# The inputs of the point network loaded in four parts behind the batch loop, with the first part's first pass placed among the last batch's gather matmuls

## What is computed

```
idx   = top_k(2 p.p - |p|^2 - |q|^2, 30)          # 30 nearest neighbours of every point
rel   = pts[idx] - pts                            # 3 coordinates, to spherical (rho, theta, phi)
feat  = [sph, sph - mean(sph)]
h     = lrelu(bn(feat @ W1.T)); h = lrelu(bn(h @ W2.T)); h = lrelu(bn(h @ W3.T))
att   = softmax(h[..., 0]);  out = x + sum_k x[idx] * att
```

## Time and profile before

| | |
|---|---|
| median of 3 runs | 7017.76 us (6999.0 to 7027.35) |
| the profiled execution | 6984.93 us, its span 6983.1 us |
| loop ends, last transposes | about 5316 to 5326 us |
| last batch's 12 groups | about 5326 to 5412 us |
| first pass, parts 0 to 2, then part 3 | 5416 to 5484 us, 5513 to 5539 us |
| rest of the network and aggregation | 5539 us to the end |
| PE, DVE busy | 6195.4 us (89%), 6047.0 us (87%) |
| mean granted clock of TensorE | 0.95 |

### The profile page before, as it was taken

One profiled execution on the slowest core, in us unless ns is written; L12 is line 12 of the kernel. 1 busy time (PEld: TensorE's weight loads), 2 busy tenths in 40 slices (PEclk: granted clock), 3 DMA queues, 4 the chain that ended last, 5 costly groups with the idle time before them and its releaser, 6 DMA issues.

```text
span 6983.1 us, 208271 instructions
## 1 busy us (share of the span) xinstructions
PE 6195.4 (89%) x79430; PEld 4459.4 (64%) x79430; DVE 6047.0 (87%) x8509; ACT 4321.9 (62%) x10325; POOL 2693.2 (39%) x3399
## 2 busy tenths in 40 slices
PE   8999999999999999999999999999995795888888
PEld 4666666666666666666666666666664234888878
DVE  6999999989999999999999999999996578777776
ACT  4666666666666666666666666666662156666666
POOL 2444444454444444444444454444443101111110
PEclk9999999999999999999999999999997898999999
DMA  3222222222222222222222222222224003222222
GB/s 118 76 75 72 71 71 68 69 75 80 76 72 78 72 68 68 72 75 76 71 72 68 69 72 83 72 75 75 75 70 133 21 16 76 63 64 62 64 66 59
DMA packets 301388, 499.32 MB, mean 72 GB/s; under 512 B 103859, under 2 KB 217699, under 8 KB 299683
## 3 DMA queue, kind: packets, MB, share of 16 engines
q1 hardware_dynamic: 246733, 389.60, 18.3%
q10 hardware_dynamic: 53589, 95.21, 4.3%
HBM read 410.45 MB, written 74.30 MB: 69 GB/s over the span
## 4 chain that ended last, share of the span: by engine, by line
DVE 41%; PE 29%; issue 21%; DMA 5%; ACT 2%; DVEq 1%; SPq 0%; POOL 0%; ACTq 0%; POOLq 0%
DVE pd L1680 10%; DVE m L1670 9%; DVE idx L1676 8%; PE SCA L901 7%; PE PD L1137 6%; DVE mx L1692 4%; PE SCA L1124 3%; DMA gat<-low_scratch 3%; DVE gat L1624 3%; PE SCB L1124 3%; DVE gat L1994 2%; PE SCB L733 2%; PE SCA L1042 1%; PE SCB L1042 1%; PE TP L1050 1%
## 5 line engine op out<-in xcount | busy, mean ns | idle before, releaser
L1670 DVE MAX8 m<-pd 128x8 f32<-128x1024 f32 x1024 | 1244.3, 1220 | 154.5 <-issue 72.1
L1676 DVE FIND_INDEX8 idx<-m,pd 128x8 uint32<-128x1024 f32 x1024 | 1245.2, 1218 | 0.0
L529 POOL TENSOR_TENSOR prod<-prod,hm 128x480 f32<-128x480 f32 x384 | 396.2, 1032 | 1934.8 <-ACT prod L1310 1923.9
L1680 DVE MATCH_REPLACE8 pd<-m,pd 128x1024 f32<-128x1024 f32 x768 | 928.2, 1209 | 0.4
L1192 ACT ACTIVATE pd<-PD,xxcol 128x512 f32<-128x512 f32 x514 | 368.7, 717 | 722.3 <-PE PD L684 692.3
L708 PEld LDWEIGHTS MISC<-ptab,gat 128*128 128x128 bf16 x23400 | 642.3, 96 | 177.7 <-DVE gat L1624 87.7
L1994 DVE TENSOR_TENSOR gat<-maskT,con 120x2048 f32<-120x2048 f32 x256 | 584.0, 2322 | 166.8 <-PE SCA L1124 164.9
L708 PE MATMUL MISC<-ptab,gat 128*128 128x24 bf16 x23400 | 653.2, 174 | 80.8 <-DVE gat L1624 78.3
L1290 ACT ACTIVATE S<-SCA,mx 128x64 f32<-128x64 f32 (+1 forms) x2560 | 590.1, 406 | 118.7 <-DVE mx L1692 118.3
L1290 ACT ACTIVATE S<-SCB,mx 128x64 f32<-128x64 f32 (+1 forms) x2560 | 580.4, 387 | 19.9 <-DVE mx L1692 19.9
L683 PE MATMUL PD<-arena 128*128 128x512 f32 x1028 | 552.6, 619 | 33.0 <-ACT pd L1192 28.3
(11 more groups left out here) (272 smaller groups left out, 14188.3 us busy)
## 6 DMA issues: line engine op xcount, KB each, us to landing
gat<-low_scratch SPq DMA_DIRECT2D x396, 640.0 KB, 3.9
arena<-in_ctx ACTq DMA_DIRECT2D x33, 512.0 KB, 4.2
x_scratch<-arena ACTq DMA_DIRECT2D x33, 512.0 KB, 3.2
x3T_scratch<-reg ACTq DMA_DIRECT2D x33, 512.0 KB, 3.4
maskT<-in_mask SPq DMA_DIRECT2D x32, 512.0 KB
arena<-in_x ACTq DMA_DIRECT2D x32, 512.0 KB, 4.4
reg<-in_ctx ACTq DMA_DIRECT2D x32, 512.0 KB, 3.5
arena<-x3T_scratch SPq DMA_DIRECT2D x32, 512.0 KB, 6.0
```

Source lines behind the costliest of these rows:

```text
L1670: V.max(m, buf[:, :]).then_inc(found, 1)
L1676: last = V.max_index(idx[:, t, 8 * r:8 * r + 8], m, buf[:, :])
L1680: V.match_replace(buf[:, :], m, buf[:, :], -3.0e38).then_inc(found, 1)
```

## The change

SP instead of ACT issues the constants and parts 0 to 2, and each part has its own semaphore. Part 0 goes out in the last round, behind that round's last index load, when the last use of Wq is done. The constants go out once the last use of `kexp` is done (the wait is on `oproj_ready`). Parts 1 and 2 go out behind the last batch's 12 index loads. DVE prepares `L1w` before the gather. On both engines the 12 chunks of part 0 are placed at the gather: four before the first fill, then one behind each of the fills 0 to 7. `divide(NB)` moves to group 6, `divide(NB + 1)` behind the statistics of part 1.

```diff
--- before.py
+++ after.py
@@ -27,6 +27,7 @@
 OHROWS = GROWS // GROUPS
 ROUNDER = 12582912.0
 DVE_STEPS = 18
+AHEAD = 4
 
 
 def program(nc, x_in, ctx_in, mask_in, w_in, b_qkv, w_out, wq, wk, wv, wo, at, bq, bk, bv, bo,
@@ -210,6 +211,7 @@
             "rel_step", "side_step", "turn_step", "div_in", "div_done"))
 
 
+        part_ld = [sem(f"part_ld{q}") for q in range(PARTS)]
         mlp_ld, stat_in, stat_ps, tstd_done, coef_done, h3_st, att_ld, att_lin, att_in, att_exp = (sem(n) for n in (
             "mlp_ld", "stat_in", "stat_ps", "tstd_done", "coef_done", "h3_st", "att_ld", "att_lin", "att_in", "att_exp"))
         l1_ready, l1_seen, h1_lin, h1_done, l2_ready, h2_done, a2_lin, a2_done, l3_ready, l3_seen, h3_done = (
@@ -241,7 +243,7 @@
         def load_part(eng, q):
 
             eng.dma_start(arena[0:GR, q * PCOLS:(q + 1) * PCOLS],
-                          sph_dram[q, :, :, :, :, :].rearrange("c f g p w -> (c f g) (p w)")).then_inc(mlp_ld, 16)
+                          sph_dram[q, :, :, :, :, :].rearrange("c f g p w -> (c f g) (p w)")).then_inc(part_ld[q], 16)
 
         LV, HV = 16, 64
         UC = 64
@@ -338,7 +340,14 @@
                                  halves[0, :, h, :].partition_broadcast(3)).then_inc(mask_ld, 16)
                 sp.dma_start(maskT[:, :], mrow[0, :].partition_broadcast(P)).then_inc(mask_ld, 16)
                 spread(i, (i + NB - 1) % NB, (i + NB - 3) % NB)
+            sp.wait_ge(pair_ready, 4 * NB)
+            sp.wait_ge(sph_st, 16 * NB)
+            load_part(sp, 0)
+            sp.wait_ge(oproj_ready, 3 * NB)
+            sp.dma_start(MK, mlp_k).then_inc(mlp_ld, 16)
             spread(NB, NB - 1, NB - 3)
+            for q in range(1, PARTS - 1):
+                load_part(sp, q)
             store_spherical(NB, NB - 2)
             store_spherical(NB + 1, NB - 1)
 
@@ -1034,14 +1043,21 @@
             split(NB)
             pe.wait_ge(split_evac, NB + 1)
             pe.wait_ge(tab_done, NB * 2 + 2)
-            for n in range(GROUPS):
-                fill(NB, n, (MISC, PD)[n % 2], 1)
-
             def first_layer(n, u):
                 for h in range(2):
                     last = mm(SC[u][0:GR, h * CW:(h + 1) * CW], L1w[:, h * GR:(h + 1) * GR], chan(GR, n, CW),
                               start=True, stop=True)
                 last.then_inc(l1_ready, 1)
+
+            pe.wait_ge(coef_done, 1)
+            pe.wait_ge(part_ld[0], 16)
+            for n in range(PCH):
+                if n >= AHEAD:
+                    fill(NB, n - AHEAD, (MISC, PD)[(n - AHEAD) % 2], 1)
+                pe.wait_ge(l1_seen, n + 1)
+                first_layer(n, n % 2)
+            for n in range(PCH - AHEAD, GROUPS):
+                fill(NB, n, (MISC, PD)[n % 2], 1)
 
             def second_layer(n, u):
                 pe.wait_ge(h1_done, n + 1)
@@ -1071,12 +1087,9 @@
                         pe.wait_ge(l1_seen, i * 2 + u + 1)
                         first_layer(i * 2 + u, u)
 
-            pe.wait_ge(coef_done, 1)
-            if PARTS > 1:
-                pe.wait_ge(mlp_ld, 16 * PARTS)
-                first_pass(0, (NCH - PCH) // 2)
-            pe.wait_ge(mlp_ld, 16 * (PARTS + 1))
-            first_pass((NCH - PCH) // 2, NCH // 2)
+            for q in range(1, PARTS):
+                pe.wait_ge(part_ld[q], 16)
+                first_pass(q * PCH // 2, (q + 1) * PCH // 2)
             norm_sums(0)
 
             pe.wait_ge(coef_done, 2)
@@ -1483,13 +1496,6 @@
             act.wait_ge(tab_done, NB * 2 + 2)
             act.dma_start(table_dram[NB - 1, :, :].rearrange("(t p) r -> p t r", p=P), tab).then_inc(table_st, 16)
             split_evacuate(NB)
-
-            act.wait_ge(x3_st, 16 * (NB + 1))
-            act.wait_ge(table_st, 16 * (NB + 1))
-            act.wait_ge(sph_st, 16 * (NB + 1))
-            act.dma_start(MK, mlp_k).then_inc(mlp_ld, 16)
-            for q in range(PARTS - 1):
-                load_part(act, q)
             for b in (NB, NB + 1):
                 roots(act, b)
                 angles(act, b)
@@ -1843,22 +1849,42 @@
                 dve.wait_ge(dve_step, NB * DVE_STEPS + tail[0])
 
             step = step_tail
+            dve.sem_inc(l1_seen, 2)
+            dve.sem_inc(h2_done, 2)
+            dve.wait_ge(mlp_ld, 16)
+            V.tensor_tensor(L1w, k1[:, 0, :], k1[:, 1, :], ALU.add)
+            step(V.tensor_tensor(k1[:, 2, :], k1[:, 2, :], k1[:, 3, :], ALU.add))
+            step(V.tensor_tensor(k1[:, 2, :], k1[:, 2, :], k1[:, 4, :], ALU.add))
+            step(V.scalar_tensor_tensor(L1w, k1[:, 2, :], -1.0 / 3.0, L1w, ALU.mult, ALU.add))
+            dve.sem_inc(coef_done, 1)
+
+            def stats(n, u):
+                dve.wait_ge(l1_ready, n + 1)
+                settle(dve)
+                for h in range(2):
+                    last = V.bn_stats(hstat[0:GR, h, bass.ds(n * 6, 6)], SC[u][0:GR, h * CW:(h + 1) * CW])
+                last.then_inc(l1_seen, 1)
+
+            def first_stats(lo, hi):
+                with dve.Fori(lo, hi) as i:
+                    for u in range(2):
+                        stats(i * 2 + u, u)
+
+            for n in range(AHEAD):
+                stats(n, n % 2)
             onehot(NB, 0)
             for n in range(GROUPS):
                 if n + 1 < GROUPS:
                     onehot(NB, n + 1)
                 consume(NB, n, (MISC, PD)[n % 2])
-            divide(NB)
-
-
-            dve.sem_inc(l1_seen, 2)
-            dve.sem_inc(h2_done, 2)
-            dve.wait_ge(mlp_ld, 16 * PARTS)
-            V.tensor_tensor(L1w, k1[:, 0, :], k1[:, 1, :], ALU.add)
-            step(V.tensor_tensor(k1[:, 2, :], k1[:, 2, :], k1[:, 3, :], ALU.add))
-            step(V.tensor_tensor(k1[:, 2, :], k1[:, 2, :], k1[:, 4, :], ALU.add))
-            step(V.scalar_tensor_tensor(L1w, k1[:, 2, :], -1.0 / 3.0, L1w, ALU.mult, ALU.add))
-            dve.sem_inc(coef_done, 1)
+                if n == 6:
+                    divide(NB)
+                if n + AHEAD < PCH:
+                    stats(n + AHEAD, n % 2)
+            for q in range(1, PARTS):
+                first_stats(q * PCH // 2, (q + 1) * PCH // 2)
+                if q == 1:
+                    divide(NB + 1)
 
             def batch_norm(l, rows, out_rows, g, b):
 
@@ -1883,21 +1909,6 @@
                 step(V.tensor_tensor(shift_l, b[0:out_rows, :], dev[0:out_rows, 0:w], ALU.subtract))
                 dve.sem_inc(coef_done, 1)
 
-            def first_stats(lo, hi):
-                with dve.Fori(lo, hi) as i:
-                    for u in range(2):
-                        n = i * 2 + u
-                        dve.wait_ge(l1_ready, n + 1)
-                        settle(dve)
-                        for h in range(2):
-                            last = V.bn_stats(hstat[0:GR, h, bass.ds(n * 6, 6)], SC[u][0:GR, h * CW:(h + 1) * CW])
-                        last.then_inc(l1_seen, 1)
-
-
-            if PARTS > 1:
-                first_stats(0, (NCH - PCH) // 2)
-            divide(NB + 1)
-            first_stats((NCH - PCH) // 2, NCH // 2)
             dve.wait_ge(l1_seen, NCH + 2)
             batch_norm(0, GR, GR, g1, b1)
```

## The result

The changed kernel ran in 6914.33 us (median of 4 runs, 6903.92 to 6923.75) against 7022.56 us for the kernel before (4 runs, 6999.0 to 7035.49): ratio 0.9858, 95% interval 0.9832 to 0.9884. The forecast was 6952 us, range 6926 to 6984.

What follows compares the result with a forecast made beforehand. Between loop and first pass's end, three things stood needlessly in a row: loads against loads, first pass behind gather, last load behind first pass. Removing 65.8 us from the 7017.8 us median gave 6952 us, range 6926 to 6984.

Steps and rivals of the forecast that it cites:

- four chunks and their statistics: Ahead of the gather, PE's first four chunks of part 0 at half clock: 11.9 us, ending at 5338.6 us.
- PE at part 1: After the last fills, PE stands 12 us until part 1 lands at 5392.8 us, then starts cold.
- PE at part 3: In the first pass, PE's first chunk of part 3 comes 27.5 us after the division, at 5447.0 us.
- The sum of 65.8 us: First pass's end moves from 5539.5 to 5473.7 us, so the whole kernel gains 65.8 us.
- The full clock through the gather: PE keeps full clock over eight steps of one fill and one chunk: 3.7 us a step, 29.6 us.
- Rival 1: PE stays at 1.2 GHz through the gather: gain only 51.6 us, 6966 us; chance 0.18.
- rival 2: Part 0 in the last round holds ACT's load, up to 10 us: 6962 us; chance 0.10.
- rival 3: Parts 1 and 2 land together, part 1 16.5 us later: gain 49 us, 6969 us; chance 0.08.
- rival 4: At the gather, two in-order queues wait for each other, 6.9 us a step: gain 40, 6978 us; chance 0.05.
- Rival 5: Altered programs lengthen each of the 32 rounds; 3.5 us a round would give 7064 us, slower than before; chance 0.03.
- the 33 us of the profiled execution under its median: Whole kernel: profiled execution 6984.9 us against median 7017.8, taken as scatter, so the forecast was set on the median.
- low end: Whole kernel: 6952 less 3 for held clock at part 3, 3 for quicker steps and loads, 20 for scatter: 6926 us.

Runs made afterwards that it cites:

- before_long: Kernel before with only PE's first-pass text rewritten (first 12 chunks written out, rest in two loops), same work, waits and order: ratio 0.9971 to before, aggregation 1099.5 us.
- the second comparison: Kernel before and changed kernel both measured again, unchanged: 6927.77 against 7014.16 us, ratio 0.9877 (0.9856 to 0.9898).

## Why the prediction was wrong, point by point

**The stretch behind the loop was right.** Counted from the last output sum (forecast / measured): part 0 issued -39.6 / -39.7; PE's first chunk 9.8 / 9.6; four chunks and their statistics 21.7 / 20.5; parts 1 and 2 issued 56.1 / 54.0; PE at part 1 75.9 / 74.8; `divide(NB + 1)` 102.6 / 100.9; PE at part 3 130.1 / 128.4; statistics 156.8 / 154.7. The sum of 65.8 us measured 67.9 in that pair of profiles and 69.9 in the second. The steps come out one by one within 2.2 us, so the sum is not right by errors that cancel.

**The full clock through the gather** held: two fills start 3.30 us apart with a chunk between them, where 3.7 was taken. It needed one more cold start, a chunk of 3.75 us behind fill 0, ahead of which PE had been idle for 2.60 us. The chunks between the later fills took 1.96 us. The Trainium skill's rule on waits between bursts ("TensorE: Matmul & The Clock Gate", "HAM oscillation — how this bites in real kernels") applies to the bursts, and the trace agrees: the first chunk of part 1, behind a wait of 13.24 us, took 3.77 us and that of part 3, behind 6.37 us, 3.76. It does not apply to the fills between chunks, where PE did not wait. Rival 1 fell with the step of 3.30 us, rival 2 by ACT's square, rival 3 by PE's start at part 1, and rival 4 by the step too.

**The step that failed is the one that was not made.** The prediction read "only the stretch from 5316 to 5539 us", since the change "leaves the 32 rounds' work and all behind the first pass's end alone". It leaves the work alone, but not the place of the code. PE's program got longer by 36 instructions as built, and the aggregation's loop lost a pause that it had in each pair of rounds, 1.5 us of each run of the final sum: 1097.2 and 1097.4 us against 1113.8 and 1111.2, about 15 us. The prediction had put this term at nothing. before_long had it without the change, so PE's program text is the cause; why a given text makes PE stop stays open. Rival 5 looked for such an effect, gave it 0.03 and only the slower side, and set it in the 32 rounds; it was in the other loop, and on the faster side. The waits view of before had the row, PE waiting for "issue" in the middle of a run of matmuls, and it was not read.

**The rest is scatter.** 68 to 70 and 15 are 83 to 85 us, and the second comparison, with 6 and 23 runs, measured 86. The first, with 4 and 4, measured 108; its interval reaches down to 81. Its 6914 lies 38 us under the forecast 6952: 2 from the stretch, 15 from the aggregation and 21 that only this comparison shows. The 15 alone would have left the time inside the range; the missed term and the scatter together carried it out. The profiles differ most in the loop: its last sum lies between 5313.7 and 5343.5 us in the 14 profiles, and a longer round goes with a lower granted clock. So the prediction was right to take the 33 us of the profiled execution under its median "as scatter", but its low end then allowed only 20 for it.

## What to carry to other kernels

A change that lengthens an engine's program moves the code behind it: compare the stretches it does not touch as well. Where one changed, write the unchanged kernel's program in the changed one's shape before crediting the edit, as before_long does; padding of the same length went the other way. Before placing work between waits, try it with the loads alone; here the moved loads, constants and divisions made the whole gain of the first pass, and the interleaving none. Compare stretches counted from a common event rather than whole executions when the loop ahead of them scatters by more than the effect.

## What the runs showed of the hardware

36 semaphore increments ahead of a loop on TensorE cost 61 us in the total (7064.7 against 7003.82 us on the same chip). In the changed kernel the same 36 cost the aggregation 25 us, so most of it is not their own work. On the queue named "instruction" packets of 16,384 bytes, 0.9 to 1.8 us each, came 5 or 6 to nearly every round of the aggregation, so a loop's code seems to be brought again in every pass; PE's 59 stops in the table ended 1.2 to 1.6 us behind such a packet. The mean granted clock of a loop round varied between 0.92 and 0.96 for the same instructions, and two neighbouring rounds at 0.93 and 0.96 took 167.2 and 163.9 us.
